# Making the FFN input of a layer's own tiles from their transposed mix input, on one Trainium2 core

## The chip, the core and the metric

The program runs on one core of a Trainium2 chip. The metric is the device time of one execution in microseconds (us); less is better. The median of the kernel before is 893.0 us over three runs. All engines of the core run their own instruction streams, in order, and meet at semaphores: TensorE (PE in the rows; PEld is its weight load), VectorE (DVE), ScalarE (ACT), GpSimd (POOL), and SyncE (SP), which here issues every DMA.

## The reference, cut to what matters

One layer of a small recurrent language model: a time-mix attention and an FFN (a ternary-weight linear layer) read the same input, and both are added to it. The input x is 8 batches of 1024 tokens by 512 channels, in float32.

```python
xn = layernorm(x, eps=1e-5)                        # per token, over 512 channels
# attention
xs = shift_by_one_token(xn)
xm = xn * time_mix + xs * (1 - time_mix)
k = exp(min(xm @ Wk.T, 60)); v = xm @ Wv.T; r = xm @ Wr.T
wkv, sum_k = decayed sums over the tokens of k*v and of k   # a scan along the tokens
attn = (sigmoid(r) * wkv / sum_k) @ Wo.T
# FFN, on the same xn
mu, var = mean(xn), var(xn)                        # per token
z = (xn - mu) * rsqrt(var + 1e-3) * ln_gamma + ln_beta
gamma = max(abs(z))                                # over the whole tensor
ffn = clip(z * 128 / gamma) @ ternary(weight) * scale
out = x + attn + ffn
```

The second normalisation works on tokens that are normalised already. Its result differs from xn by one factor per token, rsqrt(var + 1e-3), where var is the variance of the normalised token; after that come gamma and beta per channel.

## The kernel before, in words

The 8 batches are split into halves: phase A does the attention of batches 0 to 3 and prepares FFN inputs, phase B does the attention of batches 4 to 7 and all the FFN products (their scale needs the maximum over all tokens). A batch has two tiles of 512 tokens. In phase A each pass b (0 to 3) works on the batch's own tiles (own0, own1) and on the two tiles of batch b+4 (other0, other1), whose FFN inputs it prepares too. A tile is normalised with tokens on the partitions (`normalise`: two of four 128-token chunks on POOL, L1170, two on ACT, L664), then transposed by TensorE into channels-on-partitions, 128 channels at a time.

Such a transposition is a slot: four 128x128 matmuls against an identity into one PSUM bank (`transpose_slot`, L461), followed by ScalarE's evacuation of the bank (`evacuate`, L595) and by VectorE's work on it (`mix_or_clip`, L869). A pass has 24 slots n in the order of SLOT_KINDS (L44): ffn_own0 (0 to 3), ffn_other0 (4 to 7), mix_own1 (8 to 11), ffn_own1 (12 to 15), ffn_other1 (16 to 19), mix_next0 (20 to 23, the mix input of the next pass's first tile). An own tile thus passes through TensorE twice: once normalised with eps 1e-5 for the mix input, once normalised a second way for the FFN. For an FFN slot ScalarE writes z = gamma * bank + beta into one of four ring buffers `U[n % 4]` (L625), VectorE takes its largest absolute value (`absmax`, L905), and SyncE stores it to memory for phase B. For an "other" slot ScalarE first writes a plain copy as well (L624).

The main work of a pass is 24 groups g: group g = 3c + m is the projection k, v or r (m = 0, 1, 2) of chunk c, 12 matmuls of 128x512 (L513 to L515; each float32 product is made of three matmuls on high and low parts). Chunks 0 to 3 are the four channel blocks of tile 0, chunks 4 to 7 those of tile 1. On PE slot g stands ahead of group g (at g = 12, and in the first six groups of the first pass, behind it). After group 12 and at the end of the pass `attn_out` (L518) multiplies by Wo, 48 matmuls.

The order of each engine is written out by hand in its `batch` function, step by step in g:

- ScalarE (L752) in step g: `evacuate` slot g, a normalisation if one is due (NORMALISE_AT, L683: other0 at g = 2, mix_own1 at 6, other1 at 14, mix_next0 at 18; ffn_own1 at 11 and ffn_own0 at the end of the pass, L789 and L807), then `exp_k` at m = 0, followed by `ln_sums` and, later, `quotient`; `exp_r` and a logarithm at m = 2.
- VectorE (L1022) in step g: `mix_or_clip` of slot g (absmax for an FFN slot), tile statistics at g = 4, 12 and 16, `clamp_k` and `denominator` at m = 0, `rwkv` and `recurrence` (L961; one multiply, two scans, one combined multiply-add over 128x1024) at m = 1, `rwkv_lo` at m = 2.
- GpSimd (`batch_a`, L1220): the small per-token statistics (`mix_scale`, `ffn_scale`, `other`), its half of the normalisations.
- SyncE (`batch_a`, L343): stores of slots as they come, loads of the next tiles, and `store_row` (L333): a row of 512 per-token factors, 4 bytes each, which phase B loads back as one row spread over all 128 partitions (L340).

PSUM is full: three banks for k, v and r, four for the output products, one for the slots (which also borrow the last output bank).

## Time and profile before

| what | value |
|---|---|
| median of the runs | 893.0 us |
| the profiled execution: its time | 891.49 us |
| its span, first to last instruction | 889.7 us |
| PE busy | 867.1 us (97%), 3984 matmuls |
| DVE busy | 764.8 us (86%) |
| ACT busy | 510.3 us (57%) |
| POOL busy | 215.2 us (24%) |
| granted TensorE clock | 1.00 in all 40 slices |

The busy time is an average over two phases: phase A takes the span's first half, phase B the second. What a change in phase A is worth has to be read in a pass of phase A. Durations of neighbouring instructions overlap a little at their ends, so the distance from one start to the next is what an engine in a row of work really spends.

### The profile page before, as it was taken

The page shows a single profiled execution, that of the slowest core. Times are in us where ns is not written, and L with a number is a line of the kernel's source. Part 1 is how long each engine was busy: PE and PEld are TensorE (multiplying, and loading weights), DVE is VectorE, ACT ScalarE, POOL GpSimd, SP SyncE. Part 2 cuts the span into 40 slices and gives each one's busy share as a digit, 9 for nine tenths or more (in the row PEclk, how much of TensorE's full clock was granted, in tenths as well). Part 3 has the DMA queues.
Part 4 walks back from the last instruction along what each step waited for, and adds up shares of the span by engine and source line. Part 5 has one row for each costly group of instructions (what it writes and reads, how often), then busy time and mean ns, then how long its engine had stood idle before and what let it go on. Part 6 is the DMA issues. An engine that isn't in the chain of part 4 may idle for free.

```text
span 889.7 us, 12792 instructions
## 1 busy us (share of the span) xinstructions
PE 867.1 (97%) x3984; PEld 714.5 (80%) x3984; DVE 764.8 (86%) x1278; ACT 510.3 (57%) x834; POOL 215.2 (24%) x242
## 2 busy tenths in 40 slices
PE   3989999999999999999999999999999999999998
PEld 2778888888888888888888888888888888888886
DVE  5998999989897999989897897878978888789684
ACT  5584767667594757566564554545546536365441
POOL 5552326242452425240030100200201103011000
PEclk9999999999999999999999999999999999999999
DMA  8222415041423224045643245324451443424311
GB/s 283 108 83 88 149 54 184 13 171 54 165 71 135 101 82 154 12 172 136 212 145 115 84 154 189 125 75 141 153 175 57 157 141 96 154 93 142 95 48 47
DMA packets 59841, 107.13 MB, mean 120 GB/s; under 512 B 7712, under 2 KB 7712, under 8 KB 59808
## 3 DMA queue, kind: packets, MB, share of 16 engines
q1 hardware_dynamic: 59808, 106.73, 35.1%
q8 instruction: 16, 0.26, 0.1%
q14 instruction: 17, 0.14, 0.1%
HBM read 64.76 MB, written 41.96 MB: 120 GB/s over the span
## 4 chain that ended last, share of the span: by engine, by line
PE 90%; DVE 3%; issue 2%; POOL 2%; ACT 1%; DMA 0%; SPq 0%; POOLq 0%; DVEq 0%; ACTq 0%
PE kvr L513 18%; PE kvr L515 18%; PE kvr L514 18%; PE out_banks L552 7%; PE out_banks L554 7%; PE out_banks L534 6%; PE out_banks L533 6%; PE out_banks L531 6%; PE transposed L466 2%; PE out_banks L466 2%; DVE bn_stats L842 1%; POOL normed L1174 1%; POOL own_stats L1156 1%; POOL own_stats L1157 1%; DMA x<-in_x 0%
## 5 line engine op out<-in xcount | busy, mean ns | idle before, releaser
L1247 POOL TENSOR_TENSOR evacuated<-normed,mix_over_ffn_row 128x512 f32<-128x512 f32 x28 | 49.0, 1751 | 339.0 <-DVE ffn_lo L922 339.0
L513 PE MATMUL kvr<-xm_hi,wk_hi 128*128 128x512 f32 x256 | 103.7, 405 | 2.6 <-DVE xm_lo L922 2.6
L513 PE MATMUL kvr<-xm_hi,wv_hi 128*128 128x512 f32 x256 | 102.9, 402 | 2.2 <-DVE wv_lo L927 1.3
L513 PE MATMUL kvr<-xm_hi,wr_hi 128*128 128x512 f32 x256 | 102.7, 401 | 0.0
L515 PE MATMUL kvr<-xm_hi,wk_lo 128*128 128x512 f32 x256 | 101.0, 395 | 0.0
L514 PE MATMUL kvr<-xm_lo,wk_hi 128*128 128x512 f32 x256 | 100.7, 394 | 0.0
L515 PE MATMUL kvr<-xm_hi,wv_lo 128*128 128x512 f32 x256 | 100.2, 391 | 0.0
L515 PE MATMUL kvr<-xm_hi,wr_lo 128*128 128x512 f32 x256 | 100.1, 391 | 0.0
L531 PE MATMUL out_banks<-wo_hi,rwkv_hi 128*128 128x512 f32 x256 | 100.0, 390 | 0.0
L534 PE MATMUL out_banks<-wo_hi,rwkv_lo 128*128 128x512 f32 x256 | 99.7, 389 | 0.0
L514 PE MATMUL kvr<-xm_lo,wr_hi 128*128 128x512 f32 x256 | 99.7, 389 | 0.0
L514 PE MATMUL kvr<-xm_lo,wv_hi 128*128 128x512 f32 x256 | 99.7, 389 | 0.0
L552 PE MATMUL out_banks<-w_ternary,ffn_hi 128*128 128x512 f32 x256 | 99.6, 389 | 0.0
L533 PE MATMUL out_banks<-wo_lo,rwkv_hi 128*128 128x512 f32 x256 | 99.6, 389 | 0.0
L554 PE MATMUL out_banks<-w_ternary,ffn_lo 128*128 128x512 f32 x256 | 99.6, 389 | 0.0
L724 ACT ACTIVATE gate<-kvr 128x512 f32<-128x512 f32 x64 | 37.9, 593 | 90.7 <-PE kvr L515 90.7
L983 DVE SCALAR_TENSOR_TENSOR k_and_kv<-k_and_kv,constants,scans 128x1024 f32<-128x1024 f32 x64 | 83.3, 1302 | 1.1
L976 DVE TENSOR_TENSOR_SCAN scans<-constants,state,k_and_kv 128x512 f32<-128x512 f32 x64 | 79.7, 1286 | 0.0
L976 DVE TENSOR_TENSOR_SCAN scans<-constants,k_and_kv 128x512 f32<-128x512 f32 x64 | 75.8, 1226 | 0.0
L662 ACT ACTIVATE ffn_hi<-evacuated 128x512 fp32r<-128x512 f32 x64 | 39.9, 624 | 48.5 <-DVE evacuated L908 46.2
L1174 POOL TENSOR_SCALAR normed<-x,own_stats 128x512 f32<-128x512 f32 x34 | 55.0, 1623 | 51.2 <-PE out_banks L466 26.1
L922 DVE TENSOR_TENSOR ffn_lo<-evacuated,ffn_hi 128x512 fp32r<-128x512 f32 x64 | 43.9, 687 | 25.4 <-ACT ffn_hi L662 25.1
(140 smaller groups left out, 1922.7 us busy)
## 6 DMA issues: line engine op xcount, KB each, us to landing
other<-ffn_input SPq DMA_DIRECT2D x64, 256.0 KB, 5.1
x<-in_x SPq DMA_DIRECT2D x15, 1024.0 KB, 5.8
other<-in_x SPq DMA_DIRECT2D x8, 1024.0 KB, 5.8
ffn_input<-evacuated SPq DMA_DIRECT2D x32, 256.0 KB, 4.4
ffn_input<-parked SPq DMA_DIRECT2D x32, 256.0 KB, 2.2
attn_scratch<-x SPq DMA_DIRECT2D x8, 1024.0 KB, 4.2
parked<-attn_scratch SPq DMA_DIRECT2D x8, 1024.0 KB, 6.7
out<-parked SPq DMA_DIRECT2D x8, 1024.0 KB, 5.2
```

What stands on the lines that cost most here:

```text
L513: nc.tensor.matmul(KVR[:, m, :], hi, XH[t][:, ch, :], start=(ch == 0), stop=False)
L514: nc.tensor.matmul(KVR[:, m, :], hi, XL[t][:, ch, :], start=False, stop=False)
L515: last = nc.tensor.matmul(KVR[:, m, :], lo, XH[t][:, ch, :], start=False, stop=(ch == CH - 1))
L531: nc.tensor.matmul(OUT[:, q, :], hi, WH["o"][:, j, :], start=(j == 0 and ph == "A"), stop=False)
L533: nc.tensor.matmul(OUT[:, q, :], hi, WL["o"][:, j, :], start=False, stop=False)
L534: last = nc.tensor.matmul(OUT[:, q, :], lo, WH["o"][:, j, :], start=False, stop=(j == CH - 1))
L552: nc.tensor.matmul(OUT[:, q, :], AH[:, ch, q * P:(q + 1) * P], WQ[:, ch, :], start=(ch == 0), stop=False)
L554: last = nc.tensor.matmul(OUT[:, q, :], AL[:, ch, q * P:(q + 1) * P], WQ[:, ch, :], start=False, stop=(not own_tile and ch == CH - 1))
L976: last = V.tensor_tensor_scan(S[:, i, 1:TILE + 1], dec, kv[:, i, :], 0.0 if t == 0 else state[:, j, i:i + 1], ALU.mult, ALU.add)
L983: V.scalar_tensor_tensor(kv, kv, first[:, j:j + 1], S[:, :, 0:TILE], ALU.mult, ALU.add).then_inc(dve_sum, 1)
L1174: last = G.tensor_scalar(dst[:, q, :], src[:, q, :], stats[:, 2 * ffn, q:q + 1], stats[:, 2 * ffn + 1, q:q + 1], ALU.mult, ALU.add)
L1247: G.tensor_tensor(U[:, n % RING, :], XN[:, ch, :], BC[:, :], ALU.mult).then_inc(pool_v, 1)
```

## The change

An own tile is transposed once. The FFN slots of own tiles (0 to 3 and 12 to 15) are no longer made by TensorE: when ScalarE evacuates a mix slot, it also writes the bare transposed values into a new buffer Y (`own_normed`). VectorE multiplies Y by a row with one factor per token (`ffn_over_mix_rows`), spread over all partitions, and writes the product to `U`; ScalarE applies gamma and beta in place; the rest is as before. The row of factors comes from GpSimd's statistics, goes to memory as 512 values of 4 bytes and is loaded back as a row for each partition. The normalisation of own tiles for the FFN and its two last statistics steps are gone. VectorE's product for slot g+1 stands at the end of step g; that for slot 0 stands at the end of the pass before, ahead of the statistics of other0.

```diff
 def evacuate(b, ph, n, copy_own=True):
+    virtual = ph == "A" and is_virtual(n)
+    if virtual:
+        act.wait_ge(dve_z, virtual_before(b, n) + 1)
-    if ph != "B":
-        act.wait_ge(pe_t, m + 1)
+    elif ph != "B":
+        act.wait_ge(pe_t, pe_slots_before(b, ph, n) + 1)
...
     elif mix:
         if ph != "P":
+            if copy_own:
+                nc.scalar.activation(Y[:, ch, :], bank, ACT.Copy)
             nc.scalar.activation(U[:, r, :], bank, ACT.Copy, scale=tmx[:, ch:ch + 1])
...
-        nc.scalar.activation(U[:, r, :], bank, ACT.Identity, bias=bet[:, ch:ch + 1],
+        nc.scalar.activation(U[:, r, :], U[:, r, :] if virtual else bank, ACT.Identity,
+                             bias=bet[:, ch:ch + 1],
                              scale=gam[:, ch:ch + 1]).then_inc(act_u, 1)
...
+def own_ffn_input(b, n):
+    kind, ch = SLOTS[n]
+    t = int(kind[-1])
+    dve.wait_ge(s_rrow[t], 16 * b + 16)
+    if t:
+        dve.wait_ge(act_u, slots_before(b, "A", first_slot("mix_own1") + ch) + 1)
+    else:
+        dve.wait_ge(act_first, 1)
+        dve.wait_ge(act_u, slots_before(b, "A", first_slot("mix_next0") + ch - len(SLOTS)) + 1)
+    V.tensor_tensor(U[:, n % RING, :], Y[:, ch, :], RROW[:, t, :], ALU.mult).then_inc(dve_z, 1)
...
                         if c != CH - 1:
                             recurrence(b, c)
+                    if ph == "A" and is_virtual(g + 1):
+                        own_ffn_input(b, g + 1)
...
                 add_out(b, ph, "attn1")
                 if ph == "A" and not last_a:
+                    own_ffn_input(b + 1, 0)
                     tile_stats(b + 1, ph, "other0", is_last)
...
-                            if ph == "A":
-                                normalise(b, ph, "ffn_own1")
...
-                elif ph == "A":
-                    normalise(b + 1, ph, "ffn_own0")
...
-                step(i, "A", 7, G.tensor_tensor(st[:, 4, :], st[:, 3, :], half_neg[:, :], ALU.pow))
-                step(i, "A", 8, G.tensor_tensor(dst[:, 2, :], st[:, 4, :], dst[:, 0, :], ALU.mult))
-                step(i, "A", STEPS, G.tensor_tensor(dst[:, 3, :], st[:, 5, :], dst[:, 2, :], ALU.mult))
+                step(i, "A", STEPS, G.tensor_tensor(ratio[:, t, :], st[:, 3, :], half_neg[:, :], ALU.pow))
+                pool.sem_inc(pool_ratio, 1)
...
+            def store_ratio(b, t):
+                sp.wait_ge(pool_ratio, 2 * b + t + 1)
+                sp.dma_start(ratio_row[b, t].rearrange("(q p) -> p q", p=P), ratio[:, t, :],
+                             allow_slow_non_contiguous=True).then_inc(s_ratio[t], 16)
+            def load_ratio(b, t, reader_done):
+                sp.wait_ge(s_ratio[t], 16 * b + 32)
+                sp.wait_ge(dve_z, reader_done)
+                sp.dma_start(RROW[:, t, :], ratio_row[b, t].rearrange("(o n) -> o n", o=1)
+                             .to_broadcast([P, TILE])).then_inc(s_rrow[t], 16)
...
                 store_row(b, 0)
+                store_ratio(b, 1)
+                load_ratio(b, 1, virtual_before(b, CH))
                 store_ffn_input(b, 12)
```

On VectorE, early in a pass: from the combined multiply-add of chunk 0 (`k_and_kv<-k_and_kv,constants,scans`) to the `denominator` of chunk 0 (`gate<-gate,k_and_kv`). Before, the two absmax of slots 2 and 3 stand one behind the other:

```order
L983 SCALAR_TENSOR_TENSOR k_and_kv<-k_and_kv,constants,scans 128x1024
L874 REGISTER_ALU
L905 TENSOR_REDUCE absmax<-evacuated 128x1
L874 REGISTER_ALU
L905 TENSOR_REDUCE absmax<-evacuated 128x1
L957 REGISTER_ALU
L958 TENSOR_SCALAR k_and_kv<-k_and_kv 128x512
L988 TENSOR_TENSOR gate<-gate,k_and_kv 128x512
```

Now, at the same place, each absmax has the product of its own slot right ahead of it:

```order
L1041 SCALAR_TENSOR_TENSOR k_and_kv<-k_and_kv,constants,scans 128x1024
L1086 TENSOR_TENSOR evacuated<-own_normed,ffn_over_mix_rows 128x512
L932 REGISTER_ALU
L963 TENSOR_REDUCE absmax<-evacuated 128x1
L1085 REGISTER_ALU
L1086 TENSOR_TENSOR evacuated<-own_normed,ffn_over_mix_rows 128x512
L932 REGISTER_ALU
L963 TENSOR_REDUCE absmax<-evacuated 128x1
L1015 REGISTER_ALU
L1016 TENSOR_SCALAR k_and_kv<-k_and_kv 128x512
L1046 TENSOR_TENSOR gate<-gate,k_and_kv 128x512
```

Between a product and its absmax there is no other instruction of VectorE's; ScalarE's gamma-and-beta step on the same buffer lies between them in time. Slots 1, 13, 14 and 15 read the same way.

On VectorE, after the first `attn_out` of a pass: from the four additions of its result to x, with slot 13 behind them. Before:

```order
L1014 TENSOR_TENSOR x<-x,out_banks 128x512 x4
L874 REGISTER_ALU
L905 TENSOR_REDUCE absmax<-evacuated 128x1
L966 TENSOR_TENSOR k_and_kv<-k_and_kv,kvr 128x512
L971 COPY scans<-state 128x2
```

Now:

```order
L1072 TENSOR_TENSOR x<-x,out_banks 128x512 x4
L1086 TENSOR_TENSOR evacuated<-own_normed,ffn_over_mix_rows 128x512
L932 REGISTER_ALU
L963 TENSOR_REDUCE absmax<-evacuated 128x1
L1024 TENSOR_TENSOR k_and_kv<-k_and_kv,kvr 128x512
L1029 COPY scans<-state 128x2
```

The product of slot 13 stands between the additions and the absmax, and the multiply that begins chunk 4's recurrence (`k_and_kv<-k_and_kv,kvr`) has moved behind both.

## Rows read from the trace of the kernel before

**Rows 1.** The page's chain that ended last, by engine.
```profile
PE 90%; DVE 3%; issue 2%; POOL 2%; ACT 1%; DMA 0%; SPq 0%; POOLq 0%; DVEq 0%; ACTq 0%
```

**Rows 2.** Windows: one pass; us, busy of PE, PEld, DVE, ACT, POOL, clock, DMA, GB/s.
```profile
141.44:240.30 98.86, 98.76 (x482) 81.34 (x481) 90.37 (x158) 66.28 (x108) 39.23 (x48) 1.00 0.31 107
```

**Rows 3.** Timeline of PE: start, duration, instruction; a slot, then groups 11 and 12.
```profile
160.95 0.60 PE L466 MATMUL out_banks<-ident,normed 128*128 128x128 f32 x4
...
164.13 0.39 PE L513 MATMUL kvr<-xm_hi,wk_hi 128*128 128x512 f32 x1
...
166.86 0.60 PE L466 MATMUL transposed<-ident,normed 128*128 128x128 f32 x4
```

**Rows 4.** Timeline of DVE at the start of pass 2; in brackets the idle time before.
```profile
225.60 2.47 DVE L842 BATCH_NORM_STATS2 bn_stats<-other 128x6 f32<-128x512 f32 x4
...
228.94 0.69 DVE L905 TENSOR_REDUCE absmax<-evacuated 128x1 f32<-128x512 f32 x1 [0.27 <-DVE absmax_all L1104]
...
229.87 0.68 DVE L905 TENSOR_REDUCE absmax<-evacuated 128x1 f32<-128x512 f32 x1
230.99 0.69 DVE L966 TENSOR_TENSOR k_and_kv<-k_and_kv,kvr 128x512 f32<-128x512 f32 x1 [0.43 <-PE kvr L515]
...
235.66 1.27 DVE L905 TENSOR_REDUCE absmax<-evacuated 128x1 f32<-128x512 f32 x2
```

**Rows 5.** Timeline of ACT at the same place.
```profile
231.34 0.78 ACT L625 ACTIVATE evacuated<-transposed,constants 128x512 f32<-128x512 f32 x1 [2.28 <-PE transposed L466]
232.01 1.51 ACT L677 ACTIVATE other<-other,other_stats 128x512 f32<-128x512 f32 x2
234.09 0.60 ACT L724 ACTIVATE gate<-kvr 128x512 f32<-128x512 f32 x1 [0.57 <-PE kvr L515]
...
235.35 0.76 ACT L625 ACTIVATE evacuated<-out_banks,constants 128x512 f32<-128x512 f32 x1
237.30 0.60 ACT L720 ACTIVATE k_and_kv<-kvr 128x512 f32<-128x512 f32 x1 [1.19 <-PE kvr L515]
```

**Rows 6.** The chain in order of time: start, us, what; same place.
```profile
224.46 0.44 PE transposed L466 x4
...
240.30 2.47 DVE bn_stats L842 x4
```

**Rows 7.** Timeline of DVE after the first `attn_out` of pass 1.
```profile
177.42 2.45 DVE L1014 TENSOR_TENSOR x<-x,out_banks 128x512 f32<-128x512 f32 x4
179.78 0.68 DVE L905 TENSOR_REDUCE absmax<-evacuated 128x1 f32<-128x512 f32 x1
181.62 0.69 DVE L966 TENSOR_TENSOR k_and_kv<-k_and_kv,kvr 128x512 f32<-128x512 f32 x1 [1.17 <-PE kvr L515]
...
185.99 0.68 DVE L905 TENSOR_REDUCE absmax<-evacuated 128x1 f32<-128x512 f32 x1
...
191.01 2.46 DVE L842 BATCH_NORM_STATS2 bn_stats<-x 128x6 f32<-128x512 f32 x4
```

**Rows 8.** Windows of the mix slots of pass 1, columns as in rows 2.
```profile
158.00:166.00 8.00, 8.00 (x41) 6.62 (x39) 8.00 (x18) 8.00 (x15) 4.24 (x2) 1.00 0.00 0
```

**Rows 9.** Lines by form: gamma and beta from SBUF in phase B; us, mean ns.
```profile
L634 ACT ACTIVATE evacuated<-other,beta_beta,gamma_beta 128x512 f32<-128x512 f32 x32 | 25.7, 803 | 0.0
```

**Rows 10.** POOL's power step of own1 in pass 1 (timeline).
```profile
152.74 1.01 POOL L1166 TENSOR_TENSOR stat_work<-stat_work,minus_half 128x4 f32<-128x4 f32 x1 [0.18 <-POOL stat_work L1165]
```

**Rows 11.** The row store, line L335: time from issue to landing.
```profile
DMA to landing us min/median/max: 8.4/11.1/11.8
```

**Rows 12.** The page's DMA issues: KB each, median us to landing.
```profile
ffn_input<-parked SPq DMA_DIRECT2D x32, 256.0 KB, 2.2
```

**Rows 13.** DVE in pass 1: the multiply that now follows slot 12's product (timeline).
```profile
165.95 0.67 DVE L966 TENSOR_TENSOR k_and_kv<-k_and_kv,kvr 128x512 f32<-128x512 f32 x1
```

**Rows 14.** PE's first projection, after its wait at the start (timeline).
```profile
18.89 0.63 PE L514 MATMUL kvr<-xm_lo,wk_hi 128*128 128x512 f32 x1
19.32 0.63 PE L515 MATMUL kvr<-xm_hi,wk_lo 128*128 128x512 f32 x1
```

More of the change, by code:

```diff
@@ L154, in mixed_decay_kernel @@
         s_bc = sem("row_loaded")
+        s_ratio = [sem(f"ratio_row_stored{t}") for t in range(2)]
+        s_rrow = [sem(f"ratio_row_loaded{t}") for t in range(2)]
         s_mix = sem("mix_input_loaded")
@@ L221, in slots_before, with is_virtual, pe_slots_before, virtual_before @@
             return n if ph == "P" else CH + len(SLOTS) * b + n
+        def is_virtual(n):
+            return SLOTS[n][0].startswith("ffn_own")
+        def pe_slots_before(b, ph, n):
+            if ph == "P":
+                return n
+            per_batch = sum(not is_virtual(k) for k in range(len(SLOTS)))
+            return CH + per_batch * b + sum(not is_virtual(k) for k in range(n))
+        def virtual_before(b, n):
+            return 2 * CH * b + sum(is_virtual(k) for k in range(n))
         def ffn_stores_before(b, n):
@@ L251, in normed_count @@
             if ph == "A":
-                return 4 * b + [k for k in SLOT_KINDS if "other" not in k].index(kind) + 1
-            return 4 * HALF + 2 * (b - HALF) + ["mix_own1", "mix_next0"].index(kind) + 1
+                return 2 * b + ["mix_own1", "mix_next0"].index(kind) + 1
+            return 2 * HALF
         def stats_number(b, ph, tile):
@@ L288, in shifted @@
             return E[:, n % 2, :] if ph == "P" and n > 1 else WS[:, n % 2, :]
-        first_banks = [TB[:, :]] + [KVR[:, i, :] for i in range(3)]
+        first_banks = [OUT[:, q, :] for q in range(Q)]
         def slot_bank(ph, n):
@@ L356, in batch_a @@
                 sp.dma_start(X[0][:, :, :], x_t[b + 1, 0]).then_inc(s_x[0], 16)
-                for n in range(14, 19):
+                for n in range(14, 18):
                     store_ffn_input(b, n)
                 if not is_last:
-                    sp.wait_ge(pe_t, slots_before(b, "A", first_slot("ffn_other1") + CH))
+                    store_ratio(b + 1, 0)
+                store_ffn_input(b, 18)
+                if not is_last:
+                    sp.wait_ge(pe_t, pe_slots_before(b, "A", first_slot("ffn_other1") + CH))
                     sp.dma_start(ZA[:, :, :], x_t[b + HALF + 1, 0]).then_inc(s_oth, 16)
@@ L363, in batch_a @@
                 store_row(b, 1)
+                if not is_last:
+                    load_ratio(b + 1, 0, virtual_before(b, len(SLOTS)))
                 if is_last:
@@ L563, in batch @@
                     n = slot_ahead(g, is_last)
-                    if ph == "B":
+                    if ph == "B" or n is not None and is_virtual(n):
                         n = None
@@ L672, in normalise @@
                 ffn = kind.startswith("ffn")
[L674 to L675 removed]
+                i = stats_number(b, ph, tile)
+                act.wait_ge(pool_step, STEPS + steps_before(i, ph) + (OTHER_STEPS if "other" in kind else MIX_STEPS))
                 for q in ACT_CHUNKS:
@@ L707, in _ @@
                 high_part(0, "P", m)
-            act.wait_ge(pool_step, STEPS + STEPS)
-            for q in ACT_CHUNKS:
-                last = nc.scalar.activation(XN[:, q, :], X[0][:, q, :], ACT.Identity,
-                                            bias=own[:, 0, 3, q:q + 1], scale=own[:, 0, 2, q:q + 1])
-            last.then_inc(act_xn, 1)
             weight_hi("r")
+            for ch in range(CH):
+                last = nc.scalar.activation(Y[:, ch, :], first_banks[ch], ACT.Copy)
+            last.then_inc(act_first, 1)
             act.wait_ge(dve_w, 3 * CH)
@@ L757, in batch @@
                     part1_first = ahead_of_part2(n)
+                    keep = not (last_a and n is not None and SLOTS[n][0] == "mix_next0")
                     if part1_first:
-                        evacuate(b, ph, n)
+                        evacuate(b, ph, n, keep)
                     hurry = ph == "A" and g == GROUPS - 1
```

65 lines of the change are left out of this document (37 added, 28 removed).

## The prediction

> **What bounds the kernel now.** I read the chain that ended last first, then the windows of one pass of phase A, then the timelines of the three computing engines. The chain runs for 90% of the span over TensorE [rows 1], and in a pass of 98.86 us TensorE is busy for 98.76 [rows 2]: it is the bound. But VectorE works for 90.37 us of the same pass [rows 2], so it has 8.5 us of room and no more, and ScalarE 66.28. The reader is to see two things there: how much TensorE can give, and that what is given is soon taken by VectorE, whose instructions stand in a fixed order and wait for other engines in the middle of it.
>
> **What is removed.** A slot with 12 matmuls takes 164.13 - 160.95 = 3.18 us, 12 matmuls without a slot 166.86 - 164.13 = 2.73 [rows 3]. A slot is worth 0.45 us of TensorE. Eight slots in each of four passes are 32 x 0.45 = 14.4 us, if TensorE stays the bound: 1.6% and the most that this change can bring. ScalarE and GpSimd also lose their second normalisations of own tiles; neither is a bound, so I count nothing for it.
>
> **What is added on VectorE, alone.** Per pass eight products of 128x512 float32. The trace has no product with both operands as here; the nearest is the multiply of the recurrence, 0.69 us by itself [rows 4]. Of two instructions of this size in a row the second starts about 0.6 after the first (a pair takes 1.27 us) [rows 4], so 8 x 0.6 = 4.8 us of VectorE per pass. That alone would still fit in the room.
>
> **What is added in waits.** The product of slot n, ScalarE's gamma-and-beta on it, and VectorE's absmax are a chain there and back. For six of the eight slots (1, 2, 3, 13, 14, 15) nothing of VectorE's stands between product and absmax, and everything behind the absmax is queued: the recurrence, `clamp_k`, the statistics. ScalarE's step takes 0.80 us from SBUF [rows 9] and a hand-over about 0.03, so such a slot holds VectorE for 0.69 + 0.03 + 0.80 + 0.03 = 1.55 us before its absmax, where it held it for nothing. I replay the two stretches with the durations of the old rows.
>
> First stretch, in the times of pass 2. The statistics of other0 start at 225.60 [rows 4]; the product of slot 0 puts 0.6 ahead of them. Its own answer is hidden by the statistics. The absmax of slot 0 moves from 228.94 to 229.54, and absmax and `clamp_k` take 229.87 - 228.94 = 0.93 [rows 4]: product 1 at 230.47, ScalarE's answer from 231.19 to 231.99, absmax 1 at 232.02, multiply of the recurrence at 232.62. It used to start at 230.99 after 0.43 of waiting for TensorE [rows 4], so this idle time is used up. The recurrence takes 235.66 - 230.99 = 4.67 [rows 4]: product 2 at 237.29, ScalarE's answer at 238.01. ScalarE's own queue now stands behind that answer: 0.67 later (232.01 - 231.34) the normalisation of other0, 1.51 by itself and some 1.41 until the next may start, then `exp_r` and its logarithm, 235.35 - 234.09 = 1.26 [rows 5]. So ScalarE answers slot 3 only at 238.01 + 0.67 + 1.41 + 1.26 = 241.35, though its product is there at 240.1, and starts the next `exp_k` 0.7 later, at 242.05. From there to the statistics of own1 nothing changes: 240.30 [rows 6] - 237.30 [rows 5] = 3.00. They start at 245.05 instead of 240.30: **4.75 us late**, with TensorE's last `attn_out` at the same time. TensorE has no way to run ahead: slot 4 needs ScalarE's half of other0 (done near 240.1), and slot 8 needs the normalised own1, which follows the statistics.
>
> Second stretch, L being what VectorE is late as the additions begin (177.42 [rows 7]). Product 13 at 179.78 + L, its answer 0.72 later, absmax 13 at 181.33 + L, the multiply 0.6 later at 181.93 + L (181.62 before, after 1.17 of waiting for TensorE, used up too). The recurrence takes 185.99 - 181.62 = 4.37 [rows 7], so product 14 at 186.30 + L, ScalarE's answer at 187.02 + L, then as above 0.67 + 1.41 + 1.26 + 0.7 + 3.00: statistics of next0 at 194.06 + L instead of 191.01 [rows 7]. **3.05 us more.**
>
> Between them: the product of slot 12 adds 0.6 (its answer hides behind a recurrence of over 4 us). The Y copies make ScalarE's part of the mix slots longer, and there it has no room: 8.00 busy of 8.00 us [rows 8]; the nearest copy to SBUF by duration is 0.6 (`exp_k` from the same kind of bank, [rows 5]), four are 2.0 with overlaps, of which some 1.0 falls into gaps ahead of that window. And the row of slot 12 may be late. GpSimd's power step ends at 152.74 + 1.01 = 153.75 [rows 10]. Then SyncE stores 512 small pieces, which took 8.4 to 11.8 us, 11.1 in the middle [rows 11], and only when they have landed may the load go out: a 256 KB transfer takes 2.2 when the queue is short [rows 12], as it is here (0.00 of DMA time in the window [rows 8]). With 0.4 for two issues the row is there at 153.75 + 0.4 + 11.1 + 2.2 = 167.45, between 164.75 and 168.15, later if the store queues behind the other row's. The product is due at 165.95 [rows 13], or about 0.8 later with the copies. The two together: 0.8 to 2.2, up to 5 with queueing; I take 1.2, since both are counted from the same instruction. The row of slot 0 goes the same way from statistics at 191.01 [rows 7] to a product due at 225.60 [rows 4], 34.6 us, where slot 12's has 165.95 - 141.44 = 24.5 [rows 2, 13]: 10 us more, so it costs nothing.
>
> The Trainium skill puts the fixed cost of one DMA at about 2 us, most of it the receipt of the last write (DMA: Bandwidth & Descriptors, "Anatomy of one DMA"). The row store shows 11.1 [rows 11], so here the measurement decides; by the page's figure the row would never be late and this term would be the 0.8 of the copies, the sum 1.6 us less.
>
> **The sum.** Per pass 4.75 + 1.2 + 0.6 + 3.05 = 9.6 us. Nothing gives it back: between the stretches VectorE had no idle time in which to catch up, and TensorE, 3.6 us lighter per pass, waits for the statistics and for the clamped k. The gain of 14.4 us is not subtracted: it is what TensorE waits. Four passes: 38.4. At the start the product of slot 0 isn't hidden (about +1), and at the end of the last pass there is none (-0.6): nothing. Phase B has no changed instruction. Against the profiled execution's own 891.5 us this gives 891.5 + 38.4 = **930 us**; the median of the runs, 893.0, is 1.5 above that execution, which I leave within the rounding of the terms. The likeliest case alone spans 914 to 946: each round trip as priced, with 4 us per pass either way for what the replay leaves out.
>
> **The rivals.** Two per cent is about what a measurement of this kernel can tell from no change.
>
> First: the answers are hidden after all. If ScalarE's answer costs VectorE nothing at the six slots, a pass pays only 4.8 us of products against the idle time that they fill: 0.43 [rows 4], 1.17 [rows 7], and two waits for `exp_k` of about 1.0 each that follow TensorE (ScalarE's own shows 1.19 [rows 5]). 4.8 - 3.7 = 1.1 per pass, 891.5 + 4.4 = 896 us, no change. It decides at the two pairs: if absmax 2 and 3 start within 0.2 us of the end of their products' slots in the queue. For it: ScalarE is busy for only 66.28 of 98.86 us [rows 2]. Against: no instruction stands between, in program order.
>
> Second, on the other side: TensorE stays the bound, 891.5 - 14.4 = 877 us. That needs VectorE's pass under 98.86 - 3.6 = 95.3 us with 90.4 + 4.8 = 95.2 of work in it [rows 2], no wait at all. It is not slower, and would still be within 2%.
>
> Third: the row of slot 12 is the worst wait. If the store lands behind the other row's 512 pieces, 4 us later than I took, each pass loses 4 more: 930 + 16 = 946.
>
> Fourth: the clock. At the start, after its first wait, matmuls of TensorE stood 19.32 - 18.89 = 0.43 us apart [rows 14] against 2.73 / 12 = 0.23 [rows 3], about the pace of 1.2 GHz rather than 2.4, though the page shows the granted clock as 1.00 throughout. In the first stretch TensorE would end group 3 at 224.46 [rows 6] + 4 x 2.73 = 235.4 and wait for slot 4 until 240.1. If it falls to the lower pace there, two groups cost 2 x 2.4 more, of which some 1.7 is slack before slot 8: 3.1 twice per pass, 930 + 25 = 955. TensorE: Matmul & The Clock Gate in the Trainium skill says just that of idle gaps between bursts ("HAM oscillation"): each burst begins cold again. By that rule it is 955; what the trace has of it is the start alone, for a pass has no pause of TensorE to show (98.76 of 98.86 us busy [rows 2]).
>
> **How the numbers follow.** The replay 0.66; answers hidden 0.14; TensorE bound 0.03; late row 0.11; clock 0.06. Slower by over 2% (above 911): nearly all of the replay (0.63) and the last two, 0.80. Within 2%: the first two rivals and that rest, 0.18. Faster by over 2%: 0.02, for TensorE's bound allows only 1.6%. The range of 8 in 10 goes from the first rival's 896 to 948, beyond the late row.
>
> **What would show it.** In the changed profile VectorE's waits have a large new group, absmax for ScalarE's evacuation, six per pass at 0.7 to 1.1 us; TensorE idles some 3 to 5 us before slot 4 and slot 16; a pass lasts about 108 us; VectorE is over 85% busy in it while TensorE falls under 90%. A wait of the product of slot 12 for the loaded row over 2 us speaks for the third rival, matmuls 0.43 apart after slot 4 for the fourth. I am wrong if a pass is under 101 us or if absmax does not wait.

## The result, and the profile after

The changed kernel takes 934.92 us (median of four runs, 934.27 to 936.95) against 892.89 for the kernel before beside it: a ratio of 1.048, 95% interval 1.0457 to 1.0503, so 42 us slower. One of the four runs of the kernel before took 2876.54 us, the other three 891.49 to 893.0; the median leaves it aside. The forecast was 930 us and slower.

Where the time went shows in the chain that ended last. First the page's chain by engine, of the changed kernel:

```profile
PE 58%; DVE 15%; issue 9%; DMA 7%; ACT 6%; POOL 4%; SPq 0%; DVEq 0%; POOLq 0%; ACTq 0%
```

Before, 90% of it lay on TensorE [rows 1]. Now 58% does; the rest passes through VectorE, the DMAs of the row, ScalarE and GpSimd, and the hand-overs between them. The windows of the second full pass, statistics of own1 to statistics of own1 (us, then busy of PE, PEld, DVE, ACT, POOL, granted clock, DMA share, GB/s):

```profile
159.93:269.03 109.10, 99.02 (x449) 80.45 (x448) 94.54 (x166) 66.92 (x112) 29.18 (x40) 0.95 0.35 102
```

The pass is 109.10 us where it was 98.86 [rows 2], 10.24 more. VectorE's work grew by 94.54 - 90.37 = 4.17, its idle time from 8.49 to 14.56, by 6.07. The added work is the smaller part, and it came on top of idle time instead of filling it.

The waits of the whole execution (engine and line, released by; us in total, times, longest):

```profile
ACT evacuated L687 <- DVE evacuated L1086: 112.3, 24, 9.3
DVE absmax L963 <- ACT evacuated L687: 37.1, 33, 2.1
PE transposed L523 <- ACT other L740: 17.4, 4, 5.1
PE out_banks L523 <- ACT other L740: 15.8, 4, 4.3
```

The first is ScalarE, which has time to spare. The second is the round trip that the prediction priced: 32.2 of the 37.1 us stand ahead of the absmax of the six slots that it names, the rest ahead of other slots. The last two are TensorE waiting ahead of slots 4 and 16. The first stretch on VectorE, in its timeline (start, duration, instruction, idle time before; this answers to [rows 4], one pass earlier):

```profile
141.19 2.46 DVE L900 BATCH_NORM_STATS2 bn_stats<-other 128x6 f32<-128x512 f32 x4
...
145.48 0.68 DVE L1086 TENSOR_TENSOR evacuated<-own_normed,ffn_over_mix_rows 128x512 f32<-128x512 f32 x1
147.18 0.69 DVE L963 TENSOR_REDUCE absmax<-evacuated 128x1 f32<-128x512 f32 x1 [1.02 <-ACT evacuated L687]
...
152.03 0.68 DVE L1086 TENSOR_TENSOR evacuated<-own_normed,ffn_over_mix_rows 128x512 f32<-128x512 f32 x1
153.72 0.69 DVE L963 TENSOR_REDUCE absmax<-evacuated 128x1 f32<-128x512 f32 x1 [1.01 <-ACT evacuated L687]
154.33 0.68 DVE L1086 TENSOR_TENSOR evacuated<-own_normed,ffn_over_mix_rows 128x512 f32<-128x512 f32 x1
157.07 0.69 DVE L963 TENSOR_REDUCE absmax<-evacuated 128x1 f32<-128x512 f32 x1 [2.06 <-ACT evacuated L687]
...
159.93 2.46 DVE L900 BATCH_NORM_STATS2 bn_stats<-x 128x6 f32<-128x512 f32 x4
...
185.66 0.69 DVE L1086 TENSOR_TENSOR evacuated<-own_normed,ffn_over_mix_rows 128x512 f32<-128x512 f32 x1 [0.30 <-DMA ffn_over_mix_rows<-ffn_over_mix]
```

From product to absmax is 153.72 - 152.03 = 1.69 us, of which 1.01 is idle. Slot 3 costs 2.06, and ScalarE's timeline at the same place says why:

```profile
152.88 0.81 ACT L687 ACTIVATE evacuated<-evacuated,constants 128x512 f32<-128x512 f32 x1 [5.74 <-DVE evacuated L1086]
153.60 1.50 ACT L740 ACTIVATE other<-other,other_stats 128x512 f32<-128x512 f32 x2
155.01 0.57 ACT L785 ACTIVATE gate<-kvr 128x512 f32<-128x512 f32 x1
155.62 0.72 ACT L788 ACTIVATE gate<-gate,one 128x512 f32<-128x512 f32 x1
156.24 0.80 ACT L687 ACTIVATE evacuated<-evacuated,constants 128x512 f32<-128x512 f32 x1
```

ScalarE waited 5.74 us for product 2, and everything behind that answer in its order (the normalisation of other0, `exp_r`, a logarithm) waited with it. Product 3 was ready at 155.0 and got its answer only at 156.24. VectorE and ScalarE hold each other up: the wait of one puts work in front of the other's next answer.

### The profile page after: what moved, and what is told of

It is laid out like the page before. It is cut to its first block, busy times and chain, and to the rows that moved or that the text cites. A ratio compares the mean times of both kernels' runs of the same rounds, so it can differ in the third digit from the quotient of the medians.

```text
span 933.4 us, 12592 instructions
## 1 busy us (share of the span) xinstructions
PE 870.0 (93%) x3856; PEld 711.8 (76%) x3856; DVE 780.8 (84%) x1310; ACT 513.2 (55%) x850; POOL 177.8 (19%) x210
## 4 chain that ended last, share of the span: by engine, by line
PE 58%; DVE 15%; issue 9%; DMA 7%; ACT 6%; POOL 4%; SPq 0%; DVEq 0%; POOLq 0%; ACTq 0%
PE kvr L570 11%; PE kvr L572 11%; PE kvr L571 11%; PE out_banks L609 6%; PE out_banks L611 6%; PE out_banks L591 4%; PE out_banks L588 4%; PE out_banks L590 4%; DVE bn_stats L900 4%; DMA ffn_over_mix<-ffn_over_mix_stat 3%; DMA ffn_over_mix_rows<-ffn_over_mix 3%; DVE scans L1034 3%; ACT evacuated L687 2%; DVE x L1072 2%; ACT other L740 1%
## 5 line engine op out<-in xcount | busy, mean ns | idle before, releaser
L1317 POOL TENSOR_TENSOR evacuated<-normed,mix_over_ffn_row 128x512 f32<-128x512 f32 x28 | 51.2, 1829 | 336.9 <-DVE ffn_lo L980 336.9
L570 PE MATMUL kvr<-xm_hi,wv_hi 128*128 128x512 f32 x256 | 106.8, 417 | 2.8 <-DVE wv_lo L985 2.5
L571 PE MATMUL kvr<-xm_lo,wv_hi 128*128 128x512 f32 x256 | 104.0, 406 | 0.0
L572 PE MATMUL kvr<-xm_hi,wv_lo 128*128 128x512 f32 x256 | 103.7, 405 | 0.0
L687 ACT ACTIVATE evacuated<-evacuated,constants 128x512 f32<-128x512 f32 x32 | 25.9, 811 | 112.3 <-DVE evacuated L1086 112.3
L963 DVE TENSOR_REDUCE absmax<-evacuated 128x1 f32<-128x512 f32 x64 | 42.9, 681 | 37.7 <-ACT evacuated L687 37.1
```

The source lines that it names most:

```text
L570: nc.tensor.matmul(KVR[:, m, :], hi, XH[t][:, ch, :], start=(ch == 0), stop=False)
L571: nc.tensor.matmul(KVR[:, m, :], hi, XL[t][:, ch, :], start=False, stop=False)
L572: last = nc.tensor.matmul(KVR[:, m, :], lo, XH[t][:, ch, :], start=False, stop=(ch == CH - 1))
L687: nc.scalar.activation(U[:, r, :], U[:, r, :] if virtual else bank, ACT.Identity, bias=bet[:, ch:ch + 1], scale=gam[:, ch:ch + 1]).then_in ...
L1317: G.tensor_tensor(U[:, n % RING, :], XN[:, ch, :], BC[:, :], ALU.mult).then_inc(pool_v, 1)
```

## The experiments

All comparisons are with the kernel before, run beside the experiment (medians 891.5 to 893.0). The question is which part of the 42 us belongs to the products' work, to the answers, to the row, to ScalarE's copies, and whether TensorE's relief can come back.

**1. The products alone.** The kernel before, with eight products per pass at the same eight places (seven in the first pass, which has no pass before it):

```diff
+def spare_product(n):
+    V.tensor_tensor(SPARE[:, n % 2, :], SPARE[:, 2, :], SPARE[:, 3, :], ALU.mult)
...
+                    if ph == "A" and g + 1 in PRODUCTS:
+                        spare_product(g + 1)
```

> The kernel before, with eight products of the same shape per pass on VectorE at the same eight places of its order, into a buffer that nobody reads; TensorE still transposes every tile twice. Theory (the answers cost, the products mostly fill idle time): 897 us, between 893 and 901: 4.8 us of products per pass against some 3.7 us of idle time at those places, 1.1 per pass. Rival A (the products' work is what costs): 4.8 per pass, 911 us or more.

Measured: 895.20 us, ratio 1.0034 (1.0022 to 1.0046), 2.7 us more, as expected. Its pass, in the same columns as above:

```profile
144.76:243.91 99.15, 99.05 (x482) 81.32 (x481) 95.19 (x166) 66.35 (x109) 41.67 (x48) 1.00 0.31 106
```

VectorE works 95.19 us here, more than in the changed kernel, in a pass that is 0.29 longer than before: the products fill idle time. The timeline shows a product and the absmax behind it with no idle time between:

```profile
140.71 0.68 DVE L1020 TENSOR_TENSOR spare<-spare 128x512 f32<-128x512 f32 x1
141.31 0.67 DVE L907 TENSOR_REDUCE absmax<-evacuated 128x1 f32<-128x512 f32 x1
```

0.60 us from one to the other, where the changed kernel takes 1.69. The work alone is not the price; what hangs on it is.

**2. and 3. The answers covered.** Products two steps ahead, and four in a row (there with a wait for the ring buffer's low part on VectorE itself). The diff, cut, is that of the first:

```diff
-                    if ph == "A" and is_virtual(g + 1):
-                        own_ffn_input(b, g + 1)
+                    if ph == "A":
+                        for z in {0: [2], 1: [3], 11: [12, 13], 12: [14], 13: [15]}.get(g, []):
+                            own_ffn_input(b, z)
...
-                    own_ffn_input(b + 1, 0)
+                    for z in range(2):
+                        own_ffn_input(b + 1, z)
```

> VectorE makes each product two steps ahead instead of one (0 and 1 at the end of the pass, 2 and 3 in steps 0 and 1, 12 and 13 at the end of step 11, 14 and 15 in steps 12 and 13), so that other VectorE work stands between a product and the absmax that needs ScalarE's answer. Theory (uncovered answers of ScalarE: in the changed kernel's second full pass 1.02 + 1.01 + 2.06 us ahead of slot 4 and 1.02 + 1.01 + 2.07 ahead of slot 16, 8.2 per pass, 4 passes): most of 33 us comes back, 905 us, between 897 and 913, and absmax waits under 1 us per pass for two of the three at least. Rival A (the eight products' own work of 4.8 per pass is the price): 925 to 935, absmax waits gone but a pass no shorter than 107. Rival B (late row): 925 to 935, product 12 waits for the row as before, 0.3 us or more. Rival C (TensorE's lower clock after its pauses): the time falls only with the pauses, which it cannot tell from the theory.

> VectorE makes all four products of a tile in a row: 0 to 3 at the end of the pass before, 12 to 15 at the end of step 11. The amount of work is that of the changed kernel, no answer of ScalarE is asked for right away except that of slot 12. Theory (uncovered answers): 900 us, between 892 and 908: a pass of VectorE is 90.4 of work before plus 4.8 of products, 95.2, plus the idle time of some 5 us that the pass before had elsewhere. Rival A (the products' work): 925 or more. Rival B (late row): four products wait for the row at one place, so no better than the two-ahead version. If ScalarE's queue (in order, with the evacuation behind exp and logarithms) is the price rather than the bare round trip, absmax 14 and 15 still wait for over 0.7 us each and it stays above 915.

Measured: 917.96 us, ratio 1.0291 (1.0269 to 1.0312), and 923.22, ratio 1.0359 (1.0327 to 1.0391). Both give time back, 17 and 12 us, and both miss their expectation. The waits for ScalarE's answers did go. Two rows of the two-ahead version's waits show what came instead (us in total, times, longest):

```profile
DVE evacuated L1086 <- DMA ffn_over_mix_rows<-ffn_over_mix: 9.2, 6, 3.1
DVE absmax L963 <- ACT evacuated L687: 7.3, 17, 0.5
```

And its timeline of VectorE around the end of the second full pass:

```profile
241.95 1.29 DVE L1086 TENSOR_TENSOR evacuated<-own_normed,ffn_over_mix_rows 128x512 f32<-128x512 f32 x2 [3.05 <-DMA ffn_over_mix_rows<-ffn_over_mix]
...
247.41 0.68 DVE L1086 TENSOR_TENSOR evacuated<-own_normed,ffn_over_mix_rows 128x512 f32<-128x512 f32 x1
248.01 0.68 DVE L963 TENSOR_REDUCE absmax<-evacuated 128x1 f32<-128x512 f32 x1
```

37.1 us of absmax waits became 7.3, and the row's 2.2 us became 9.2 (the 7.7 in expectation 5 below counts five of the six, without 1.53 in the first pass). Absmax 2 follows its neighbour without idle time, but products 0 and 1 wait 3.05 for the row. In the four-at-once version one wait for the row is 3.41, all four products stand behind it, and TensorE waits 14.4 us for GpSimd's half of the other tiles. A VectorE that comes earlier meets the row.

**4. and 5. Nobody waits for the row**, in the changed kernel and in the two-ahead version; the loads go on, into a spare buffer, and the row buffer holds 1:

```diff
-                dve.wait_ge(s_rrow[t], 16 * b + 16)
...
-                sp.dma_start(RROW[:, t, :], ratio_row[b, t].rearrange("(o n) -> o n", o=1)
+                sp.dma_start(SPARE[:, t, :], ratio_row[b, t].rearrange("(o n) -> o n", o=1)
```

> The changed kernel, but VectorE doesn't wait for the row: the row buffer is filled with 1 once at the start, and the loads of the row go, at the same places, to a buffer that nobody reads (the factor per token is left out of the FFN input). Theory (uncovered answers; the row costs only what VectorE waited for it, 2.2 us in 5 times): 932, between 929 and 935. Rival (late row, the answers merely stand where the row's wait would be): 920 or less.

> Products two steps ahead, and no wait for the row (as in the run beside it, the factor is left out). With products two ahead VectorE waited 7.7 us for the row, 3.05 of it for slot 0 of the third pass. Theory (answers first, and once they are covered the row is the next limit): 910, between 905 and 914, with passes near 102 us. If the row's wait only hid another one behind it, 915 to 919. Rival (ScalarE's copies and the products' own work are the rest): also 910, for what is left then is neither answers nor row.

Measured: 936.08 us, ratio 1.0481 (1.0453 to 1.0508), and 907.18, ratio 1.0169 (1.0143 to 1.0195). The first lies just above its range (929 to 935), the second within its own. In the changed kernel the row costs nothing that shows: the ratio is that of the changed kernel itself, although the row's DMAs hold 7% of the chain that ended last there. With the answers covered it costs 917.96 - 907.18 = 10.8 us. The same wait is free in one kernel and a quarter of the loss in another, because the answers had covered it.

**6. and 7. Rows sent sooner**, all work kept. Both also store the row for phase B of tile 0 later. The first version also put GpSimd's factors ahead of its half of the normalisation of next0; the second left GpSimd's order alone. Cut to the load of the row of slot 0:

```diff
+                    load_ratio(b + 1, 0, virtual_before(b, len(SLOTS)))
                     sp.wait_ge(pe_t, pe_slots_before(b, "A", first_slot("ffn_other1") + CH))
                     sp.dma_start(ZA[:, :, :], x_t[b + HALF + 1, 0]).then_inc(s_oth, 16)
...
                 store_row(b, 1)
-                if not is_last:
-                    load_ratio(b + 1, 0, virtual_before(b, len(SLOTS)))
```

> Products two steps ahead, and the rows sent sooner with all their work kept: GpSimd makes the factors of next0 ahead of its half of the normalisation (3 us sooner), SyncE loads the row of slot 0 before the 1 MB load of the next other tile and not behind it, and both rows of factors that phase B needs are stored behind, not ahead of, these. Theory (the row of slot 0 was late because its 256 KB stood behind a 1 MB load and 512 small pieces in the same queue): it lands 8 us sooner, product 0 waits for nothing, product 12 under 0.5 us, total as without the wait, 910, between 905 and 915. If the row is late by its own way through memory (8 to 9 us store, 5 us load), both waits stay and it is 917 or more. The 1 MB load goes 4 us later: if the statistics of other0 then wait for it, 915 to 925.

> Products two steps ahead; GpSimd's order as in the changed kernel (in the run with rows sent sooner, its later half of the normalisation made TensorE and VectorE wait 4.2 us for slot 20); SyncE loads the row of slot 0 ahead of the 1 MB load of the next other tile, and stores the row of phase B for tile 0 only behind the store of slot 12, so that neither its 512 pieces nor the 1 MB stand in the way of a row of factors. Theory (the row is the second limit, and its lateness is queueing): 910, between 905 and 915, row waits under 2 us per pass together. If the row's own way through memory (8 us store, 5 us load) is the limit: 915 or more with over 3 us of row waits per pass.

Measured: 925.95 us, ratio 1.0373 (1.0352 to 1.0394), and 916.88, ratio 1.0262 (1.0232 to 1.0292). The first is a miss on the wrong side: GpSimd began its normalisation 10.6 us after the statistics of next0 and not 5.9, TensorE waited 3.46 us for it ahead of slot 20 and VectorE 4.21 behind that, and product 12 waited 2.99 for its row, whose load took 7.2 with 512 pieces now issued right behind it. The second is no faster than the two-ahead version, the intervals overlap. The loads of the row, in the view of their line, first of this second version:

```profile
DMA to landing us min/median/max: 3.8/5.4/6.9
```

Then of the two-ahead version:

```profile
DMA to landing us min/median/max: 4.3/5.1/15.1
```

So the longest load did stand behind the 1 MB and the 512 pieces (which of the two, this doesn't tell), and no longer does. The waits for the row fell from 9.2 to 5.9 us. Product 0 waits for nothing any more; the four waits that are left are all at product 12, whose load already followed its store directly: the store takes 8.8 to 10.3, the load behind it 5.4. So queueing was the price at slot 0, and the row's own way through memory is what is left at slot 12. The expectation is met by halves: under 2 us of row waits per pass, as its first case says, but the time of its second. Which wait took the place of these 3.3 us is not shown.

**8. Without ScalarE's copies**, in the changed kernel:

```diff
-                        if copy_own:
-                            nc.scalar.activation(Y[:, ch, :], bank, ACT.Copy)
...
+            V.memset(Y[:, :, :], 1.0)
```

> The changed kernel without ScalarE's copies of the transposed mix input (the buffer is filled with 1 at the start, so the FFN input of own tiles is made of the factors alone); all products, answers and rows stay. Theory (the copies cost what VectorE waited for ScalarE in the mix slots, 0.19 + 0.64 + 0.19 = 1.0 per pass): 931, between 928 and 934. Rival (ScalarE's longer queue is what makes its answers late): 925 or less. No effect at all, 934 to 937, would say that the row or another wait is right behind.

Measured: 946.29 us, ratio 1.0605 (1.0587 to 1.0624): less work, and 11.4 us slower than the changed kernel, outside every case of the expectation. VectorE's waits:

```profile
DVE absmax L960 <- ACT evacuated L685: 37.1, 33, 2.1
DVE evacuated L1083 <- DMA ffn_over_mix_rows<-ffn_over_mix: 17.6, 8, 3.0
```

The answers cost what they cost before, to the tenth. The row cost 17.6 instead of 2.2: 15.4 more, against the 3.3 that the changed kernel waits for ScalarE in the mix slots in all. That leaves 12.1, near the 11.4. The stores of the row took 8.9 us in the middle here and 8.1 in the changed kernel, the longest load 14.9 and 13.5. In the second full pass product 12 was due 0.8 us sooner after the statistics and its row landed 1.0 later. Why the stores took longer with less work around them is open; nothing tried here tells it. What it shows is how close the changed kernel stands to the row: product 12 waits 0.26 to 0.74 us for it in each pass already.

**9. to 11. Products on GpSimd**, to give VectorE its time back: as such, with the rows sent sooner, and with nobody waiting for the rows.

```diff
+                pool.wait_ge(dve_lo, slots_before(b, "A", n) + 1)
-                V.tensor_tensor(U[:, n % RING, :], Y[:, ch, :], RROW[:, t, :], ALU.mult).then_inc(dve_z, 1)
+                G.tensor_tensor(U[:, n % RING, :], Y[:, ch, :], RROW[:, t, :], ALU.mult).then_inc(dve_z, 1)
```

> GpSimd makes the products in place of VectorE (a 128x512 product of GpSimd from two SBUF buffers takes 1.83 us in phase B of the changed kernel, 14.6 us per pass beside 29 busy of 109), four in a row, 12 to 15 after its statistics of own1 and 0 to 3 after those of next0. Theory: VectorE is back at 90.4 us of work per pass, no answer is uncovered, and TensorE, 3.6 us lighter per pass, is the bound again: 885 us, between 876 and 895, faster than the kernel before by up to 1.7%. Rival A (the products' work is what cost): also under 895, it can't be told apart here. Rival B (late row): products 12 to 15 come after the row, which in the changed kernel landed 25.7 us after the statistics of own1 began, and end 7.3 us later, so absmax 12 waits 1.5 us or more in each pass: 893 to 905.

> Products on GpSimd, and the rows sent sooner as in the run beside it. With products on GpSimd the row of slot 0 landed 14.3 us after its load was issued and the products ended 7 us after the statistics of other0 were ready, so that GpSimd's share of other0 came late and TensorE waited for it; absmax 2 waited 4.2 us. Theory (late rows are what holds the GpSimd version, VectorE having its 90.4 us of work back): 905, between 893 and 915. Rival (GpSimd's products at 1.3 to 2.0 us each are themselves too slow ahead of absmax): 925 or more.

> Products on GpSimd, and nobody waits for the rows (buffer of 1, the loads go elsewhere; the factor is left out). VectorE has its 90.4 us of work per pass back and TensorE 95.2. Theory (late rows hold the GpSimd version): 890, between 878 and 902. Rival (GpSimd's own time for four products, 5.2 to 7.8 us in a row ahead of its share of other0 and other1, and of absmax, is the limit): 910 or more, with TensorE waiting for GpSimd ahead of slots 4 and 16.

Measured: 933.77 us, ratio 1.0453 (1.0399 to 1.0506); 930.16, ratio 1.0435 (1.0404 to 1.0466); 915.89, ratio 1.0264 (1.0247 to 1.0282). Three misses; the times of the rivals of the last two (925 or more, 910 or more) came. In the first GpSimd stood 131.3 us for the rows and could not get to the other tiles. Without any wait for the row it is still slower than VectorE's own two-ahead products without that wait (907.18). Of the 9.9 us between the spans of these two, 6.2 arise before the first statistics of own1: there GpSimd makes its four products only behind its work on other0, and VectorE waits once for long:

```profile
41.11 0.69 DVE L965 TENSOR_REDUCE absmax<-evacuated 128x1 f32<-128x512 f32 x1 [7.92 <-ACT evacuated L688]
```

The later passes are 0.2 to 1.9 longer than with two-ahead products. Why GpSimd's products don't bring them back to 98.86 the windows of the second full pass show:

```profile
157.11:259.86 102.75, 96.20 (x447) 77.16 (x446) 95.48 (x158) 67.37 (x112) 43.59 (x48) 1.00 0.40 108
```

VectorE has its old 158 instructions back and is busy for 95.48 us, not 90.37. VectorE's timeline in that pass:

```profile
178.36 1.79 DVE L1052 TENSOR_TENSOR k_and_kv<-k_and_kv,gate 128x512 f32<-128x512 f32 x1
180.07 1.25 DVE L957 TENSOR_TENSOR evacuated<-evacuated,last_token 128x1 f32<-128x1 f32 x1
...
239.12 1.82 DVE L1056 TENSOR_TENSOR rwkv_lo<-k_and_kv,rwkv_hi 128x512 fp32r<-128x512 f32 x1
```

GpSimd's timeline at the same times:

```profile
177.92 3.38 POOL L1291 TENSOR_TENSOR evacuated<-own_normed,ffn_over_mix_rows 128x512 f32<-128x512 f32 x2 [7.91 <-DVE xm_lo L982]
...
239.10 1.29 POOL L1291 TENSOR_TENSOR evacuated<-own_normed,ffn_over_mix_rows 128x512 f32<-128x512 f32 x1 [8.46 <-DVE xm_lo L982]
```

An instruction of 0.69 us takes 1.79 or 1.82 when it falls on a product of GpSimd, one of 0.16 takes 1.25; the last of the three ends at 240.94, 0.55 behind the end of GpSimd's product. Eight products cost VectorE 95.48 - 90.37 = 5.1 us per pass, as much as if it made them (4.8).

**12. Answers, row and copies all gone** from the path, products kept: the edits of 2, 5 and 8 together.

> Products two steps ahead, no wait for the row, and no copies by ScalarE: the answers, the row and the copies are covered or gone at once (the copied values and the factor are both a constant 1, so the FFN input of own tiles is left out), while VectorE still makes all eight products per pass and TensorE has 32 transpositions less. Theory (the three waits and the products are the whole price): with two of them gone it was 907, and VectorE still waited 0.95 + 0.64 + 0.20 = 1.8 us per pass for ScalarE in the mix slots: 900, between 896 and 903, passes near 100.7 us. It stays above 893, since VectorE's pass is 90.4 + 4.8 us of work with some idle time, where the pass before was 98.9: TensorE's relief is worth nothing even then. Rival (TensorE's relief returns once the waits are gone): 885 or less.

Measured: 902.83 us, ratio 1.0119 (1.0100 to 1.0138), within what was expected, at its upper end. The windows of its second full pass:

```profile
147.33:248.81 101.48, 97.30 (x450) 79.24 (x449) 94.77 (x167) 63.37 (x105) 32.33 (x40) 0.98 0.40 109
```

Even so the pass is 2.6 us longer than before, and TensorE's lighter load returns nothing. Set beside experiment 1, whose VectorE does the same work in 99.15, VectorE's waits for ScalarE in the pass hold 0.42 twice and 0.46 once ahead of an absmax, 0.46 and 0.20 in the mix slots and 0.48 behind `exp_k` that experiment 1 doesn't have: 2.4 us, against 2.33 by which the pass is longer. Where TensorE's relief goes its timeline shows, ahead of slots 8 and 20:

```profile
157.16 0.78 PE L524 MATMUL transposed<-ident,normed 128*128 128x128 f32 x4 [2.43 <-POOL normed L1252]
...
208.33 0.66 PE L524 MATMUL out_banks<-ident,normed 128*128 128x128 f32 x4 [1.12 <-POOL normed L1252]
```

TensorE comes earlier to these slots and waits there for GpSimd's half of the normalised tile, which follows VectorE's statistics. Behind the wait of 2.43 its granted clock is 0.76 from 156 to 159 us and 0.67 from 159 to 162; it still waits 0.55 for VectorE ahead of the next `attn_out`, so this is not read as a price, but no run was made on it.

In steps: 934.9 as changed, 918.0 with the answers covered, 907.2 without the row, 902.8 without the copies, 893 before. Of the 42 us, 934.92 - 902.83 = 32.1 are taken away by these runs. Of the last 9.9, 2.7 are the products (experiment 1); the other 7 are small waits for ScalarE like those above, read from rows and not taken away one by one. The steps were taken in this order only; experiments 4 and 8 show that in another order the same edits give nothing or less. No version tried is faster than the kernel before.

## Why the prediction was right

**What was removed.** None of the 14.4 us shortened the kernel, as said. TensorE waits 17.4 + 15.8 = 33.2 us ahead of slots 4 and 16, 4.84 and 4.01 in the two stretches read here ("3 to 5" in the prediction), and it is busy for 870.0 us where it was 867.1, with 128 matmuls fewer: those behind these waits run at the lower clock (below). The slots' worth was never in doubt; its use was.

**First stretch.** Predicted 4.75. Measured from the statistics of other0 to those of own1: 159.93 - 141.19 = 18.74, where it was 14.70 [rows 4, 6], so 4.04, and 0.60 for product 0 ahead of them, 4.64. The order in ScalarE's queue came as replayed, and so did the three answers, nearly (1.02, 1.01 and 2.06 of waiting, by the replay 0.86, 0.86 and 2.05; the sign "0.7 to 1.1" fits the first two only). The idle time that had been there, 0.43 for TensorE and about 1.0 for `exp_k`, is gone. Two parts miss and cancel: a round trip takes 1.69 and not 1.55, since ScalarE starts 0.17 after a product's end (hand-over 0.03 in the prediction), and the recurrence takes 152.03 - 147.78 = 4.25 and not 4.67.

**Slot 12.** Predicted 1.2 for copies and row together; own1 to product 12 takes 25.73, where the multiply in its place followed after 24.51 [rows 2, 13]: 1.22. The waits there are 0.30 for the row and 0.19 + 0.64 + 0.19 in the mix slots. The row was there 25.7 after the statistics, 26.0 in the prediction, and that the two agree is luck, for the parts miss both ways: the store took 8.1 and not 11.1, the load 4.5 and not 2.2, and GpSimd ended 0.6 later. The other three passes come to 0.6 to 1.5.

**Second stretch.** Predicted 3.05, measured from the additions to the statistics of next0:

```profile
197.88 2.48 DVE L1072 TENSOR_TENSOR x<-x,out_banks 128x512 f32<-128x512 f32 x4
...
211.98 0.69 DVE L963 TENSOR_REDUCE absmax<-evacuated 128x1 f32<-128x512 f32 x1 [2.07 <-ACT evacuated L687]
...
214.83 2.46 DVE L900 BATCH_NORM_STATS2 bn_stats<-x 128x6 f32<-128x512 f32 x4
```

This is 16.95, before 191.01 - 177.42 = 13.59 [rows 7]: 3.36 more here, 3.4 in the pass after, 3.8 in the first and 3.6 in the last, in both of which the stretch was shorter before. The 0.3 beyond the forecast are two hand-overs to ScalarE of 0.17 and not 0.03.

**The row of slot 0**, "10 us more, so it costs nothing": this step failed. In this pass it landed late:

```profile
249.72 0.69 DVE L1086 TENSOR_TENSOR evacuated<-own_normed,ffn_over_mix_rows 128x512 f32<-128x512 f32 x1 [0.32 <-DMA ffn_over_mix_rows<-ffn_over_mix]
```

Its load was taken at 2.2 us from a short queue, but it stands behind a 1 MB load and 512 pieces and took up to 13.5. With 0.32, once in the whole execution, the error is small here; once the answers were covered the wait was up to 3.05, and both rows together were the second largest cost (experiments 2 and 5).

**The start.** Predicted: the first stretch's 4.75, and about +1 that was then set against the end and counted as nothing. The statistics of own1 in the first pass, in the timelines of the changed kernel and then of the kernel before:

```profile
50.44 2.46 DVE L900 BATCH_NORM_STATS2 bn_stats<-x 128x6 f32<-128x512 f32 x4
```

```profile
42.44 2.46 DVE L842 BATCH_NORM_STATS2 bn_stats<-x 128x6 f32<-128x512 f32 x4
```

They are 8.0 late. This is the term that was most mis-sized, by 3.25 in the sum: VectorE had no idle time there at all, so the four waits (1.15, 1.01, 1.01 and 2.07), 0.46 ahead of the absmax of slot 4 and four products of 0.6 count in full, 8.1.

**The sum.** A pass was to be 98.86 + 9.6 = 108.46; the three full ones are 109.49, 109.10 and 108.89. From the last statistics of own1 to the end it is 4.9 more than before, 4.85 by the terms. 8.0 + 30.8 + 4.9 is the 43.7 by which the spans differ (933.4 and 889.7); the forecast's 38.4 falls short by 5.3. Of this 3.25 is the start; in the three full passes together 1.4 is the second stretch and 1.0 the part around slot 12, less 0.4 in the first stretch. One sign was too bold: VectorE is busy for 94.54 / 109.10 = 87% of the pass, as said, but TensorE for 91% rather than under 90: 99.02 us, where 98.76 - 3.6 = 95.2 would be left, since matmuls at the lower clock are longer.

**The rivals.** Answers hidden after all (896): no, absmax waits 37 us. TensorE as the bound (877): not even with three waits out of the way (902.8). Late row (946): it didn't take place in the changed kernel, where taking the wait away changes nothing. It is the next limit behind the answers (experiments 2 and 5). Experiment 8 shows late rows too, and 946.3, but by some 2 to 3 us at both rows and not 4 at one; that the times meet is chance. The clock (955): its sign came, its price did not. TensorE's timeline behind the wait ahead of slot 4:

```profile
155.25 0.88 PE L523 MATMUL transposed<-ident,other 128*128 128x128 f32 x4 [4.84 <-ACT other L740]
...
157.20 0.63 PE L570 MATMUL kvr<-xm_hi,wv_hi 128*128 128x512 f32 x1
157.63 0.63 PE L571 MATMUL kvr<-xm_lo,wv_hi 128*128 128x512 f32 x1
...
159.14 0.39 PE L572 MATMUL kvr<-xm_hi,wv_lo 128*128 128x512 f32 x1
159.37 0.40 PE L570 MATMUL kvr<-xm_hi,wv_hi 128*128 128x512 f32 x1
```

Matmuls stand 0.43 us apart, then 0.23 again; the granted clock from 155 to 160 us is 0.66 on average. About seven of them at the lower level (1.2 GHz) cost TensorE 7 x 0.2 = 1.4 us, and by the rows VectorE waited for ScalarE then, not for TensorE (0.46 ahead of the next absmax); no run was made on the clock alone. By the Trainium skill's rule that a burst after a long enough pause begins cold (TensorE: Matmul & The Clock Gate, "HAM oscillation") the event was to be expected, and the trace agrees: 0.66 behind the wait of 4.84, 1.00 behind one of 1.02 at 194.96. The price that the prediction put on it, 3.1 per stretch, was wrong because two groups were taken at the lower level and there was a good half of one.

## What to carry to other kernels

Moving work from the bounding engine to the next one is priced not by its duration but by the hand-overs that it adds: a product of 0.6 us held VectorE for 1.7 because the next instruction in VectorE's order needed another engine's answer to it, and the answer of that engine was queued in turn. Look for what stands between a request and the use of its answer, on both engines, and start the request early. And when one wait covers another, neither removal tells its price alone: take them away together as well as one by one.

## What was not expected of the hardware

A product of GpSimd with both operands in SBUF held up VectorE's instruction until it was done: 0.69 became 1.79 and 1.82, 0.16 became 1.25, and VectorE's busy time rose by 5.1 us per pass for eight of them. The Trainium skill says of the port that the two share that "it's an exclusive lock (not a bandwidth split)" (Trainium Architecture — The Big Picture, "What this means for kernel authors"); the rows agree, and the expectation of experiment 9 overlooked it.

The store of the row of factors, 512 values of 4 bytes, took 7.7 to 10.7 us from issue to landing in the versions whose traces show it, and the load of 256 KB over the partitions 4.9 to 6.3 more in the middle, up to 16.5 behind a 1 MB load and 512 pieces. That its store took 0.8 longer in the version with less work on ScalarE has no explanation here.
